# Seven gathered slots instead of six, and a scaling in four pieces, in a graph network on one core

## The chip, the core and the metric

The kernel runs on one core of a Trainium2 chip. Its engines work side by side and in order, each on its own list of instructions: TensorE (PE) multiplies, VectorE (DVE) and ScalarE (ACT) work on elements, GpSimd (POOL) issues among others the indirect transfers that gather table rows by index, and SyncE (SP) issues plain transfers. They wait for each other through semaphores. The metric is the time of one execution on the device in microseconds, the median of the runs shown.

## What is computed

Three graph layers on 3125 nodes and 53125 edges (sorted by target `dst`), a residual and a norm, then a message layer over the same edges:

```python
for l in range(3):                      # _L0_gnn_ref
    neigh = segment_sum(h[src], dst) * inv_deg
    h = h @ Ws_self[l] + neigh @ Ws_neigh[l] + bs[l]      # relu but in the last
x = layernorm(x + h)
# _L1_gnn_ref, idx_i = src, idx_j = dst
hs, hv = xs @ w_in2f_s, xv @ w_in2f_v           # a row of 4*32 values for each node
s, v = hs[idx_j], hv[idx_j]                     # gathered for each edge
Wij = (ssp(f_ij @ W1 + b1) @ W2 + b2) * rcut_ij
edge = products of s, v, the edge's angles Yr_ij and Wij
agg = segment_sum(edge, idx_i)                  # then two small products, ssp between
x = layernorm(x + out)
```

## The kernel before

Nodes are cut into TILES = 25 tiles of TN = 125. **First pass** (25 steps): products of tile and weights, and dense count matrices from the edges. **Three passes** of 25 steps each, k = 0 to 74 (AGGS = 75): TensorE multiplies the counts of tile k (25 blocks of 125 x 125, loaded into `abuf`) with the table of all nodes' rows (50 matmuls with 512 columns, L1208), and the products of the next layer lie between them. VectorE first scales the counts of tile k+1 in place, `scale(k + 1, 0)` at L1687, one operation over 3125 elements except at the first tiles of a pass, where `parts_of` (L575) cuts it. TensorE waits for a piece through `s_as` and `scaled_at`, which follows the written list SCALES (L566). In the third pass (k from 50) VectorE also takes moments (L1743 to L1763), norms (L1768, `normed`) and adds the residual (L1757); the normed rows give one tile a step of `msg_table`, which SyncE stores (L642) and counts in `s_rows`.

The edges were sorted by the tile of `src` into `by_src` during the second and third pass: each of 25 source tiles has a window of 128 partitions x SLOTS = 18 slots, sorted by `dst` within. A slot is thus a column of 128 edges, and its rows are gathered by one indirect transfer from `msg_table` by the edges' `dst`.

**Early gathers.** At the end of k = 50 POOL loads the window columns 0 to 5 of all tiles (L928, three transfers) and columns 6 to 11 of tile 0 (L926), copies the indices (L933, L934), and VectorE finds how many table tiles each slot needs (`early_max`, L1709 on, and `early_need`). TensorE waits for the maxima at k = 52, a = 4 (L1195). POOL then works through 30 steps (j, c): slot j of the five tiles of chunk c, five gathers (`gather_slot`, L937) into one of three buffers, and a store of the step before to `early_rows` (L951). A last step gathers the second group (slots 6 to 11) of tile 0 and stores it to `second_rows` (L960).

**Message stage.** For each source tile t there are NG = 3 groups of GS = 6 slots. VectorE's `group(t, g)` waits for TensorE's filters (L1220) and for the group's rows in `msg_slots[t % 2]`, makes products (L1991 first, then L1994, L1996, L2000, L2004, L2006); ScalarE scales (`scaled`, L1466), and TensorE sums (`sums`, L1242). Group 0's rows come from `early_rows` in one load (SyncE L814; ScalarE L1447 for tile 0), tile 0's group 1 from `second_rows` (L818), and all the others POOL gathers in the open (`gather`, L910), 12 a tile, 6 for tile 0, in order of tile and group, after all of `msg_table` has been stored. It may run two tiles ahead (`s_gd`).

Of the kernel before, what the change touches and what calls it, by code (L numbers as in the profile page):

```python
# [11 lines left out]
P = 128  # L12
# [12 lines left out]
SECOND = GS * CHUNKS  # L25
# [68 lines left out]
def gnn_kernel(nc, x, src, dst, src_n, pay, ws, wn, bs, w_in, w1, b1, w2, b2, wf1, wf2, out):  # L94
# [17 lines left out]
    early_rows = nc.dram_tensor("early_rows", [GS, CHUNKS, P, FEW * G], F32).ap()  # L112
    second_rows = nc.dram_tensor("second_rows", [P, GS * G], F32).ap()
# [58 lines left out]
    e_rows = [early.take(P, [GS, G]) for _ in range(3)]  # L172
    e_idx = early.take(P, [TILES, GS], I32)
    e_second = early.take(P, [GS], I32)
    e_f = early.take(P, [GS, TILES])
    e_fs = early.take(P, [GS])
    e_max = early.take(P, [GS + 1])
    e_most = early.take(1, [GS + 1])
    e_below = early.take(1, [GS + 1, TILES])
    e_need = early.take(1, [GS + 1], I32)  # L180
# [97 lines left out]
    e_win = ereg.take(P, [TILES, GS, PAY])  # L278
    e_swin = ereg.take(P, [GS, PAY])
# [128 lines left out]
    s_second = sem("second_group_loaded")  # L408
# [58 lines left out]
    def early_gathered(s):  # L467

        return 16 * sum(GS if n == SECOND else FEW for n in range(s % 3, s + 1, 3))

    def slots_gathered(t, g):

        if g == 0:
            return 16 * (t // 2 + 1)
        return 16 * GS * (t // 2 + (0 if g == 1 and t % 2 == 0 else 1))
# [99 lines left out]
    def parts_of(k):  # L575

        return {0: (0, 22, 23, 24, 25), 1: (0, 23, 25)}.get(k % TILES, (0, 25))

    with nc.Block() as block:

        @block.sync
        def _(sp):
# [147 lines left out]
            for k in range(AGGS):  # L730
# [44 lines left out]
                if k == AGGS - 4:  # L775
                    sp.wait_ge(s_eidx, len(PARTS_OF) + 1)
# [29 lines left out]
            def load_early(t):  # L806
                if t >= 2:
                    sp.wait_ge(s_gd, 3 * NG * (t - 2) + 3)
                c, i = t // FEW, t % FEW
                if t == 1 or i == 0:  # L810
                    for j in range(GS):
                        s = early_step(j, c)
                        sp.wait_ge(s_est[s % 3], loads_of(s, 3))
                sp.dma_start(msg_slots[t % 2][:, 0:GS, :], early_rows[:, c, :, i * G:(i + 1) * G].rearrange("j p k -> p j k")).then_inc(s_g[0][t % 2], 16)  # L814

            extras(sp, extra_round)
            sp.wait_ge(s_est[SECOND % 3], loads_of(SECOND, 3))
# [1332 lines left out]
```

## Time and profile before

| | us |
|---|---|
| median of 3 runs | 1892.74 (1888.39 to 1895.12) |
| the profiled execution | 1891.2 |
| its span | 1889.4 |
| PE busy | 1827.0 (97%) |
| DVE busy | 1180.4 (62%) |
| POOL busy | 1180.8 (62%) |
| ACT busy | 627.3 (33%) |

Times in the profile are from the start of the span. A "busy" share is an average over stages with different limits; the stage has to be looked at by itself. In a timeline a row gives start and duration of an instruction (or of several in a row, x6), and in brackets how long its engine had been idle and what ended that. "issue" is idle time for which the profile shows no releaser. The third pass runs from about 1142 to 1452, the message stage from 1457 to the end.

### The profile page before, as it was taken

What the parts mean: (1) busy time and instruction counts of PE and PEld (TensorE: products, weight loads), DVE (VectorE), ACT (ScalarE), POOL (GpSimd) and SP (SyncE); (2) the same over time, 40 slices, a digit from 0 to 9 for tenths busy, and PEclk for the clock granted to TensorE, in tenths of its full rate; (3) what the DMA queues carried; (4) which work ended last, traced back from release to release, by engine and by line L of the source; (5) the groups of instructions that cost most, each with busy time, mean ns of one, the idle gap of its engine ahead of it and who ended that gap; (6) DMA issues with size and microseconds to landing.
All of it is one profiled execution on the core that took longest, in us unless ns stands there. A gap on an engine that the chain in (4) does not pass through costs nothing. (4 is left out here: it accounts for less than half of the span.)

```text
span 1889.4 us, 23661 instructions
## 1 busy us (share of the span) xinstructions
PE 1827.0 (97%) x8259; PEld 1160.8 (61%) x8259; DVE 1180.4 (62%) x1811; ACT 627.3 (33%) x1432; POOL 1180.8 (62%) x1082
## 2 busy tenths in 40 slices
PE   7999999999999999999999998999998999999997
PEld 3454455555555555555555555666666888888886
DVE  5766678677644344343343344555553899999997
ACT  1566632233000000000000000111103888888885
POOL 4400000165588888888888883788886777777773
PEclk9999999999999999999999999999998999999999
DMA  5365566443454435444444434555564344434442
GB/s 156 108 218 182 202 217 185 124 115 104 129 143 138 123 107 147 134 134 124 117 130 122 114 98 156 179 190 195 195 196 133 89 116 116 113 108 107 108 117 56
DMA packets 235894, 261.88 MB, mean 139 GB/s; under 512 B 130678, under 2 KB 173280, under 8 KB 235773
## 3 DMA queue, kind: packets, MB, share of 16 engines
q1 hardware_dynamic: 200956, 204.29, 35.6%
q0 software_dynamic: 34032, 55.66, 11.0%
q8 instruction: 67, 1.10, 0.3%
q10 hardware_dynamic: 784, 0.39, 0.1%
q14 instruction: 55, 0.44, 0.1%
HBM read 172.52 MB, written 87.69 MB: 138 GB/s over the span
## 5 line engine op out<-in xcount | busy, mean ns | idle before, releaser
L1208 PE MATMUL low<-table,abuf 125*125 125x512 f16 x3750 | 835.2, 380 | 0.0
L1208 PEld LDWEIGHTS low<-table,abuf 125*125 125x125 bf16 x3750 | 506.4, 137 | 303.0 <-issue 27.9
L905 POOL DMA_INDIRECT by_src<-scat_row,sort x416 | 502.7, 1208 | 126.1 <-issue 118.8
L1037 PE MATMUL mid<-wbuf,h_t 128*125 128x512 f32 x1200 | 557.2, 601 | 14.0 <-DVE st_out L1733 10.9
L910 POOL DMA_INDIRECT table<-msg_table,wbuf x294 | 316.8, 1078 | 97.8 <-issue 97.5
L1037 PEld LDWEIGHTS mid<-wbuf,h_t 128*125 128x125 f32 x1200 | 214.9, 189 | 222.1 <-issue 198.2
L1743 DVE SCALAR_TENSOR_TENSOR y<-low,inv_deg,st_in 125x512 f32<-125x512 f32 x75 | 56.2, 749 | 446.6 <-PE low L1208 328.1
L1687 DVE TENSOR_TENSOR abuf<-abuf,row_scale 125x3125 bf16<-125x3125 bf16 (+4 forms) x87 | 256.9, 2956 | 1.2 <-DMA abuf<-adj 1.2
L937 POOL DMA_INDIRECT sort<-msg_table,sort x156 | 202.0, 1295 | 63.9 <-issue 47.2
L888 POOL TENSOR_TENSOR sort<-sort 128x416 f32<-128x416 f32 x26 | 31.8, 1224 | 329.9 <-DVE sort L1805 329.9
L1242 PE MATMUL low<-table,wbuf 128*125 128x256 f32 x900 | 209.9, 383 | 21.0 <-ACT table L1466 20.9
L1242 PEld LDWEIGHTS low<-table,wbuf 128*125 128x125 f32 x900 | 167.7, 189 | 50.1 <-DVE table L2006 25.1
L1419 ACT ACTIVATE y<-y 125x512 f32<-125x512 f32 x48 | 30.2, 629 | 437.7 <-DVE y L1743 437.7
L1332 ACT ACTIVATE table<-mid,row_inv_i 125x512 f16<-125x512 f32 x75 | 51.2, 683 | 314.2 <-DVE row_inv_i L1698 314.1
L1343 ACT ACTIVATE table<-top 125x500 bf16<-125x500 f32 (+1 forms) x175 | 120.4, 691 | 94.3 <-PE top L1068 94.2
L1466 ACT ACTIVATE table<-table,wbuf 128x128 f32<-128x128 f32 x450 | 139.3, 388 | 36.1 <-DVE table L1996 36.1
L1220 PE MATMUL mid<-w_sb,wbuf 97*128 97x384 f32 (+2 forms) x450 | 112.7, 387 | 2.4 <-issue 2.4
L1068 PEld LDWEIGHTS top<-table 128*128 128x128 bf16 x625 | 49.0, 98 | 77.6 <-issue 70.0
L1706 DVE SCALAR_TENSOR_TENSOR table<-mid,row_inv_i,table 125x512 f16<-125x512 f32 x75 | 56.3, 751 | 52.1 <-ACT table L1332 52.1
L1733 DVE TENSOR_TENSOR st_out<-mid,bias 125x512 f32<-125x512 f32 x75 | 51.4, 685 | 53.3 <-issue 49.9
L1220 PEld LDWEIGHTS mid<-w_sb,wbuf 97*128 97x128 f32 x450 | 69.4, 194 | 23.5 <-issue 3.8
L1662 DVE TENSOR_TENSOR table<-sort,node_iota 128x3200 bf16<-128x3200 bf16 (+1 forms) x45 | 81.8, 1855 | 2.0 <-ACT sort L1351 1.9
(244 smaller groups left out, 1616.6 us busy)
## 6 DMA issues: line engine op xcount, KB each, us to landing
abuf<-adj SPq DMA_DIRECT2D x75, 781.2 KB, 5.0
adj<-table SPq DMA_DIRECT2D x25, 781.2 KB, 4.5
states<-st_out SPq DMA_DIRECT2D x75, 256.0 KB, 2.3
st_in<-states SPq DMA_DIRECT2D x75, 256.0 KB, 4.9
flips<-y_flip SPq DMA_DIRECT2D x48, 256.0 KB, 4.3
h_t<-flips SPq DMA_DIRECT2D x192, 64.0 KB
early_rows<-sort POOLq DMA_DIRECT2D x30, 320.0 KB, 2.7
table<-early_rows SPq DMA_DIRECT2D x24, 384.0 KB, 6.5
```

What stands on the lines that cost most here:

```text
L905: pool.indirect_dma_start(out=by_src, out_offset=bass.IndirectOffsetOnAxis(ap=place_i[:, k * PIECE + j:k * PIECE + j + 1], axis=0), in_=sc ...
L910: pool.indirect_dma_start(out=rows[:, j, :], out_offset=None, in_=msg_table[:, :], in_offset=bass.IndirectOffsetOnAxis(ap=win[:, j, PAY_DS ...
L937: pool.indirect_dma_start(out=e_rows[s % 3][:, j, :], out_offset=None, in_=msg_table[:, :], in_offset=bass.IndirectOffsetOnAxis(ap=idx, ax ...
L1037: last = pe.matmul(to[0:TN, :], h_t[i % 2][:, k, 0:TN], weights[l % 2][:, a, k, :], start=k == 0, stop=k == KC - 1)
L1208: last = pe.matmul(p_agg[k % 2][0:TN, :], a_tile[k % 3][:, a, :], table[ps % 2][0:TN, a, h, :], start=a == 0 and h == 0, stop=a == TILES - ...
L1220: last = pe.matmul(w[:, (b * BLK + lo) * G:(b * BLK + hi) * G], filters[b], w2_sb[:, lo:hi, :].rearrange("k a b -> k (a b)"), start=True, ...
L1242: last = pe.matmul(p_acc[0:TN, :], hot32[:, g * GS + j, :], msg[n % 2][:, j, :], start=g == 0 and j == 0, stop=g == NG - 1 and j == GS - 1)
L1343: act.activation(to, of, ACT.Copy).then_inc(s_blke, 1)
L1466: last = act.activation(msg[n % 2][:, j, 0:G], av[n % 2][:, j, F:F + G], ACT.Copy, scale=win_p[t % 3][:, g * GS + j, PAY_Y:PAY_Y + 1])
L1662: return dve.tensor_tensor(to.rearrange("p b (n a) -> p b n a", a=PAIR), column.unsqueeze(2).broadcast_to([P, BLOCKS, n, PAIR]), node_iota ...
L1687: dve.tensor_tensor(a_tile[k % 3][:, lo:hi, :], a_tile[k % 3][:, lo:hi, :], row_scale[k // TILES % 2][0:TN, lo:hi].unsqueeze(2).broadcast_ ...
L1706: dve.scalar_tensor_tensor(out=table[l % 2][0:TN, t, 1, :], in0=n, scalar=row_inv[0:TN, 0:1], in1=table[l % 2][0:TN, t, 0, :], op0=ALU.mul ...
```

## The change

- `EARLY = 7`: early gathers take slots 0 to 6 of every tile, 35 steps of five gathers. The step for tile 0's second group, `second_rows`, `e_second`, `e_fs`, their load, copy, cast, reduction and semaphore go away.
- `load_early(t)` brings seven slots in one transfer, and waits for group 1 of tile t-2 where it waited for group 0, because slot 6 belongs to group 1.
- In the message stage POOL gathers slots 7 to 17 of every tile, tile 0 too: 11 a tile. Group 1's count of five gathers a tile is `2 * GS - EARLY`.
- `parts_of(k)` for k > 51 has four parts (0, 7, 13, 19, 25) in place of one. Part 0 keeps its place, part 1 follows before `normed`, part 2 before `add_residual`, part 3 behind it.

```diff
-SECOND = GS * CHUNKS
+EARLY = 7
+STEPS = EARLY * CHUNKS
...
+    def parts_of(k):
+
+        return {0: (0, 22, 23, 24, 25), 1: (0, 23, 25)}.get(k % TILES, (0, 7, 13, 19, 25) if k > 2 * TILES else (0, 25))
+
+    def later_parts(k):
+
+        return range(1, 4) if 2 * TILES + 1 < k < AGGS else range(0)
...
+        SCALES += [(k + 1, part) for part in later_parts(k + 1)]
...
             def load_early(t):
                 if t >= 2:
-                    sp.wait_ge(s_gd, 3 * NG * (t - 2) + 3)
+                    sp.wait_ge(s_gd, 3 * (NG * (t - 2) + 1) + 3)
...
-            pool.dma_start(e_swin, edges_of[:, 0, GS:2 * GS, :]).then_inc(s_ewin[0], 16)
             for n, (lo, hi) in enumerate(PARTS_OF):
                 pool.dma_start(e_win[:, lo:hi, :, :].rearrange("p t j k -> p t (j k)"),
-                               edges_of[:, lo:hi, 0:GS, :].rearrange("p t j k -> p t (j k)")).then_inc(s_ewin[n], 16)
+                               edges_of[:, lo:hi, 0:EARLY, :].rearrange("p t j k -> p t (j k)")).then_inc(s_ewin[n], 16)
...
-            steps_of = [(j, c) for j in range(GS) for c in range(CHUNKS)]
+            steps_of = [(j, c) for j in range(EARLY) for c in range(CHUNKS)]
...
-            need = pool.value_load(e_need[0:1, GS:GS + 1], min_val=1, max_val=TILES)
-            wait_alone(pool, s_rows, need)
-            gather_second()
             store_early(*steps_of[-1])
-            store_second()
...
-                for g in range(1 if t else 2, NG):
+                for g in range(1, NG):
                     if t >= 2:
                         pool.wait_ge(s_gd, 3 * (NG * (t - 2) + g) + 3)
-                    for j in range(g * GS, (g + 1) * GS):
+                    for j in range(max(g * GS, EARLY), (g + 1) * GS):
                         gather(msg_slots[t % 2], win_p[t % 3], j, s_g[g][t % 2])
...
+                for part in later_parts(k + 1)[0:1]:
+                    scale(k + 1, part)
                 if k > 2 * TILES:
                     normed(k - 1)
...
+                for part in later_parts(k + 1)[1:2]:
+                    scale(k + 1, part)
                 if ps == 2:
                     add_residual(k)
+                for part in later_parts(k + 1)[2:3]:
+                    scale(k + 1, part)
```

## Rows read from the trace of the kernel before

**Rows 1.** Windows: length, then busy time per engine, PE clock, DMA share.

```profile
1168.00:1420.00 252.00, 252.00 (x1294) 170.41 (x1293) 131.47 (x153) 26.48 (x83) 195.87 (x164) 0.99 0.56 183
1450.00:1500.00 50.00, 44.32 (x209) 36.84 (x210) 35.67 (x59) 35.73 (x91) 32.45 (x30) 0.83 0.41 116
1650.00:1700.00 50.00, 47.68 (x272) 41.03 (x271) 48.40 (x88) 42.01 (x115) 39.03 (x37) 1.00 0.42 110
```

**Rows 2.** Groups by line, 1550 to 1800: count, busy us, mean ns, idle before.

```profile
L910 POOL DMA_INDIRECT table<-msg_table,wbuf x181 | 195.5, 1080 | 55.2 <-issue 55.2
```

**Rows 3.** Timeline of a steady tile: start, duration, engine, line, idle before.

```profile
1671.66 0.75 DVE L1991 TENSOR_TENSOR table<-table,wbuf 128x576 f32<-128x576 f32 x1
...
1673.58 1.86 ACT L1466 ACTIVATE table<-table,wbuf 128x128 f32<-128x128 f32 x6 [0.87 <-DVE table L1996]
...
1675.58 2.83 PE L1242 MATMUL low<-table,wbuf 128*125 128x256 f32 x12 [0.77 <-ACT table L1466]
...
1679.56 1.47 PE L1220 MATMUL mid<-w_sb,wbuf 97*128 97x384 f32 x6
...
1681.06 0.76 DVE L1991 TENSOR_TENSOR table<-table,wbuf 128x576 f32<-128x576 f32 x1 [0.33 <-PE mid L1220]
...
1681.87 0.95 POOL L910 DMA_INDIRECT table<-msg_table,wbuf  x1 [0.30 <-issue]
...
1688.29 0.75 DVE L1991 TENSOR_TENSOR table<-table,wbuf 128x576 f32<-128x576 f32 x1
```

**Rows 4.** Timeline of the message stage's first tiles.

```profile
1462.34 2.77 PE L1220 MATMUL mid<-w_sb,wbuf 97*128 97x384 f32 x6
...
1464.83 0.95 POOL L910 DMA_INDIRECT table<-msg_table,wbuf  x1 [0.30 <-issue]
...
1469.94 2.08 POOL L910 DMA_INDIRECT table<-msg_table,wbuf  x1 [0.30 <-issue]
...
1470.46 0.74 DVE L1991 TENSOR_TENSOR table<-table,wbuf 128x576 f32<-128x576 f32 x1
...
1483.48 1.13 POOL L910 DMA_INDIRECT table<-msg_table,wbuf  x1 [0.30 <-issue]
...
1487.53 0.76 DVE L1991 TENSOR_TENSOR table<-table,wbuf 128x576 f32<-128x576 f32 x1 [2.03 <-issue]
```

**Rows 5.** Groups by line, 1168 to 1450, third pass.

```profile
L937 POOL DMA_INDIRECT sort<-msg_table,sort x156 | 202.0, 1295 | 63.9 <-issue 47.2 <-SPq L773 16.8
L951 POOL DMA_DIRECT2D early_rows<-sort x30 | 17.5, 584 | 0.0
...
L1687 DVE TENSOR_TENSOR abuf<-abuf,row_scale 125x3125 bf16<-125x3125 bf16 x22 | 75.0, 3407 | 0.0
```

**Rows 6.** Timeline of one scaling and the gather beside it.

```profile
1386.85 3.41 DVE L1687 TENSOR_TENSOR abuf<-abuf,row_scale 125x3125 bf16<-125x3125 bf16 x1
...
1387.46 3.61 POOL L937 DMA_INDIRECT sort<-msg_table,sort  x1 [0.31 <-issue]
1390.17 0.54 DVE L1768 TENSOR_SCALAR table<-y,mv,rstd 125x512 f32<-125x512 f32 x1
```

**Rows 7.** End of the early gathers: timeline, chain (start, us, what), timeline.

```profile
1450.27 0.77 POOL L960 DMA_DIRECT2D second_rows<-sort  x1 [1.19 <-DMA sort<-msg_table,sort]
...
1454.97 2.31 DMA msg_table<-msg_row
...
1459.57 1.01 POOL L910 DMA_INDIRECT table<-msg_table,wbuf  x1 [8.53 <-issue]
```

**Rows 8.** Start of the third pass: chain of waits.

```profile
1156.71 8.61 DMA wbuf<-by_src
```

**Rows 9.** Transfers of the message stage: KB each, median us to landing.

```profile
table<-early_rows SPq DMA_DIRECT2D x24, 384.0 KB, 6.5
...
table<-early_rows ACTq DMA_DIRECT2D x1, 384.0 KB, 3.6
```

**Rows 10.** L1991 alone: what ended VectorE's idle time before it (us, times).

```profile
  issue: 3.4, 4
```

More of the change, by code:

```diff
@@ L171, in gnn_kernel @@
     early = Region(sort_sb[:, :], 7 * CH * 4)
[L172 to L180, printed above, removed]
+    e_rows = [early.take(P, [FEW, G]) for _ in range(3)]
+    e_idx = early.take(P, [TILES, EARLY], I32)
+    e_f = early.take(P, [EARLY, TILES])
+    e_max = early.take(P, [EARLY])
+    e_most = early.take(1, [EARLY])
+    e_below = early.take(1, [EARLY, TILES])
+    e_need = early.take(1, [EARLY], I32)
     x_rows = Region(sort_sb[:, :], 7 * CH * 4).take(P, [SLOTS, G])
@@ L277, in gnn_kernel @@
     ereg = Region(wbuf[:, :, :].rearrange("p a k -> p (a k)"), 2 * 2 * KC * D * 4)
-    e_win = ereg.take(P, [TILES, GS, PAY])
-    e_swin = ereg.take(P, [GS, PAY])
+    e_win = ereg.take(P, [TILES, EARLY, PAY])
     treg = Region(tbuf[0][:, :], T_SIZE)
@@ L467, in early_gathered @@
     def early_gathered(s):
-        return 16 * sum(GS if n == SECOND else FEW for n in range(s % 3, s + 1, 3))
+        return 16 * FEW * (s // 3 + 1)
     def slots_gathered(t, g):
-        if g == 0:
-            return 16 * (t // 2 + 1)
-        return 16 * GS * (t // 2 + (0 if g == 1 and t % 2 == 0 else 1))
+        return 16 * (t // 2 + 1) * {0: 1, 1: 2 * GS - EARLY}.get(g, GS)
     def node_rows(t):
@@ L915, in extra_round @@
                 wait_alone(pool, s_xl, q * 32)
-                for s in range(SECOND - 2, SECOND + 1):
+                for s in range(STEPS - 3, STEPS):
                     pool.wait_ge(s_est[s % 3], loads_of(s, 3))
@@ L951, in store_early @@
                 pool.dma_start(early_rows[j, c, :, :].rearrange("p (t k) -> p t k", t=FEW), e_rows[s % 3][:, 0:FEW, :]).then_inc(s_est[s % 3], 16)
-            def gather_second():
-                pool.wait_ge(s_est[SECOND % 3], loads_of(SECOND - 3, 3))
-                for j in range(GS):
-                    gather_slot(SECOND, j, e_second[:, j:j + 1])
-            def store_second():
-                pool.wait_ge(s_eg[SECOND % 3], early_gathered(SECOND))
-                pool.dma_start(second_rows.rearrange("p (j k) -> p j k", j=GS), e_rows[SECOND % 3]).then_inc(s_est[SECOND % 3], 16)
             pool.wait_ge(s_eneed, 1)
-            steps_of = [(j, c) for j in range(GS) for c in range(CHUNKS)]
+            steps_of = [(j, c) for j in range(EARLY) for c in range(CHUNKS)]
             for n, (j, c) in enumerate(steps_of):
@@ L1193, in _ @@
                         pe.wait_ge(s_emax, 1)
-                        for n in range(GS + 1):
+                        for n in range(EARLY):
                             top = pe.transpose(p_b[n // 4][0:1, n % 4 * P:(n % 4 + 1) * P], e_max[:, n:n + 1], ident[:, :])
@@ L1443, in _ @@
             act.wait_ge(s_acc, AGGS)
-            for j in range(GS):
+            for j in range(EARLY):
                 s = early_step(j, 0)
                 act.wait_ge(s_est[s % 3], loads_of(s, 3))
-            act.dma_start(msg_slots[0][:, 0:GS, :], early_rows[:, 0, :, 0:G].rearrange("j p k -> p j k")).then_inc(s_g[0][0], 16)
+            act.dma_start(msg_slots[0][:, 0:EARLY, :], early_rows[:, 0, :, 0:G].rearrange("j p k -> p j k")).then_inc(s_g[0][0], 16)
             def hots(t):
```

35 lines of the change are left out of this document (11 added, 24 removed).

## Prediction

> **What bounds the kernel now.** I read the windows first. Through the third pass TensorE is busy 252.00 of 252.00 us, and GpSimd (POOL), which gathers rows there for later, is not what the pass waits for. In the message stage VectorE is busy 48.40 of 50 us, TensorE 47.68, POOL 39.03 [rows 1]. The chain of waits of the page gives 15% of the span to POOL's gathers at L910, so the next question is whether POOL paces the stage. The grouped view makes it look so: 181 gathers in 250 us, busy 195.5, idle 55.2 and all of that "issue", which is 0.305 us behind every gather, never a wait [rows 2].
>
> The timeline of one steady tile says otherwise [rows 3]. The last gather of tile 13's third group is issued at 1681.87 and used at 1688.29, 6.42 us later (7.52 us for the second group). Where a group really waits for its gather, the distance is 4.05 us (issued 1483.48, used 1487.53, VectorE idle 2.03 before it) [rows 4]. So in the steady part rows lie ready 2.4 us before use. What repeats every 16.63 us (L1991 at 1671.66 and at 1688.29) is another loop: VectorE's product lets ScalarE scale (1673.58, 1.86 us), then TensorE sums (1675.58, 2.83), hidden layer and filters (1679.56, 1.47) release VectorE's L1991 at 1681.06 after an idle 0.33, and VectorE works on without a pause to the next turn. POOL keeps the same 16.63 us because VectorE's operations hold it up: 12 gathers x 1.255 is 15.06, and holds fill the rest. POOL follows; it doesn't lead.
>
> **Third pass: gathers added.** 175 gathers in 35 steps stand for 156 in 31 (30 steps of five and one of six). A gather undisturbed costs 0.95 + 0.305 = 1.255, a store 0.584 + 0.3 = 0.88 [rows 5]. Added: 19 x 1.255 + 4 x 0.88 = 23.8 + 3.5 = 27.4 us of POOL.
>
> **Third pass: scaling in four.** The 156 gathers were busy 202.0 us; 156 x 0.95 is 148.2, so 53.8 us are holds, 2.4 for each of 22 scalings of 3.41 us [rows 5]. How a hold looks: the scaling L1687 runs 1386.85 to 1390.26, the gather issued at 1387.46 ends at 1391.07, 0.81 after it [rows 6]. After the change the pieces hold 875 and 750 elements; at 3.41 us for 3125 they are about 0.97 and 0.84 us, 3.5 together. VectorE's order becomes piece, piece, L1768, piece, L1757, piece, some 4.3 us in a row. The question is whether a held gather gets in between two of them or waits for all. In rows 6 L1768 (1390.17, 0.54) stands right behind the scaling; had the gather waited for it too, it would have ended at 1391.5, not 1391.07. It got in between, and so it does in all 19 cases of this kind. Then the first gather is held up to 0.97 us, the next, 1.1 us behind the end of an operation, meets the tail of one: some 0.6 to 1.0 us a step, 13 to 22 in all. If the two pieces that follow each other directly count as one (no row shows this pair), 1.7 us at the first and up to 38 in all. I take 20. POOL: +27.4 + 20 - 53.8 = -6 us (ends: -13 and +12).
>
> What this is worth: POOL ended this work at 1451.04 (1450.27 + 0.77) and then sat idle 8.53 us, because the last row of the table landed only at 1457.28 (1454.97 + 2.31); the first gather of the message stage came at 1459.57 [rows 7]. So earlier is worth nothing, and up to 6.2 us later costs nothing: **0 us**, at most 6 at the far end. TensorE gets three more waits a step, about 70; it is busy 252.00 of 252.00 with the waits it has, so 0 (bound: 0 to 1.5 us). The pieces end 1.1 us later than the one operation did, and five microseconds of VectorE's idle time follow, so TensorE's next tile doesn't see them. L1768, now ahead of two pieces, comes 1.5 us sooner and nobody is waiting for it: 0. VectorE's fixed cost of three more operations, 0.1 to 0.2 us a step, goes into the same idle time.
>
> The Trainium skill, SBUF — State Buffer, section Who interferes with whom, says that a VectorE operation with two SBUF inputs contends with a GpSimd instruction that reads SBUF, which the 19 held gathers bear out. The same section also reports `tensor_tensor` as not stalling DMAs; by that the holds would have another cause, and the split would give nothing (rival 2).
>
> **Start of the third pass.** TensorE and VectorE wait there for POOL's indices: transfers from by_src, 8.61 us from issue to the last landing, on the chain of waits [rows 8]. Bytes grow from 156 to 175 slot columns (12%): up to +1.0 us. The first of four issues falls away, and so do two small VectorE operations (L1712, L1714). No row here has their price; on VectorE nothing in this profile is under 0.15 us, so I take 0.9 for the three (0.5 for an issue like the 0.58 of a store [rows 5], 0.2 each for the others): -0.9. Sum +0.1, bounds -0.9 to +1.0.
>
> **Message stage, steady part.** POOL issues 11 gathers a tile, not 12. By rows 3 nobody waited for the twelfth: 0 us over tiles 5 to 23. The load of the seven slots now waits for the second group of tile t-2, not the first, some 5.4 us later on SyncE (a third of 16.63). Behind it in that queue stands the window load of tile t+1, which waits for the third group's sums of that same tile t-2 and so still comes later; and from there to the use in tile t are almost two tiles, over 24 us, for a load of 6.5 us [rows 9]. Hidden; if that cover were gone, 6.5 us a tile. The load on ScalarE's queue for tile 0 grows by a sixth: it took 3.6 us from 1454.91, so it lands near 1459.1 where 1458.5 was [rows 9], and VectorE starts at 1460.03 after TensorE's filters. Hidden by 0.9 us.
>
> **Message stage, first tiles: here it costs.** Before, tile 0's second group was ready in second_rows. Now POOL gathers five of its slots in the open, and until tile 5 it has more to do than before (11 + 11t gathers against 6 + 12t). I walk it with rows 4 and 7.
> - Tile 0, second group: fifth gather issued 1464.83, + 4.05 = 1468.9.
> - Tile 0, third group: six more gathers, 7.5 us, issued about 1472.4, landed 1476.5. It was used at 1470.46, so +6.0.
> - Tile 1, second group: ScalarE, TensorE's sums, hidden and filters come behind that, as in rows 3: still +6.0.
> - Tile 1, third group: VectorE's own work reaches it 5.4 us later, at 1491.5; its gathers (the 22nd) land near 1490.9. It was used at 1487.53 after the 2.03 us wait, which is now swallowed: +4.0.
> - Tile 2, third group: moves by the same 4.0. Its 33rd gather lands over 2 us before VectorE gets there. From here nobody waits for gathers any more. Before, L1991 had four waits of this kind, 3.4 us together [rows 10]; the first was the 2.03, so the three later ones are worth -1.3.
>
> That is **+2.7 us**. While TensorE waits for tile 0's second group it stands idle some 3.6 us at a moment when its clock is still mostly down (0.83 of full over 1450 to 1500 [rows 1]; the filters took 2.77 us there against 1.47 at 2.4 GHz [rows 3, 4]). Staying longer at 1.2 GHz costs from 0 to 4.1 us (one round of filters, hidden layer and sums at the slow rate, 1.3 + 1.3 + 1.5). I take 0.6, nearer to none, because most of that round then lies beside waiting for gathers.
>
> **Sum.** 0 + 0.1 + 0 + 2.7 + 0.6 = +3.4 us. The profiled execution took 1891.2 us (span 1889.4 and 1.8 around it): 1894.6 after. That execution lies 1.5 below the median of the three runs, 1892.74, so the median after should be **1896** (0.18% more). About 0.3%, 5.7 us, is what a measurement of this kernel can tell from no change.
>
> **Rivals.**
> 1. *No measurable change, slightly slower* (the forecast), 1896, own range 1890 to 1901. Chance 0.64.
> 2. *The third pass hands the delay on* (slower). If the pieces in a row hold POOL as one, or the holds aren't the scaling's, nothing of the 53.8 us is saved and POOL ends at 1451.04 + 27.4 = 1478.4. It decides from 1457.3 on: 21 us late, and VectorE can't catch up at 16.63 a tile. 21 + 2.7: 1916. Against it: 19 gathers that got in behind the scaling. One gather at 1469.94 that took 2.08 us, held by two operations in turn [rows 4], speaks for it. Chance 0.06.
> 3. *The first tiles cost more* (slower by over 0.3%): low clock until tile 1 (+4.1 for +0.6), or POOL ready only at 1461 (+4). 1900 to 1903. For it: the clock in rows 1; against: most of that slow round lies beside waiting for gathers. Chance 0.18.
> 4. *POOL paces the stage after all* (faster). The page's chain and the unbroken row of gathers speak for it, the 6.42 us against it. With 11 gathers a tile would fall to VectorE's busy time, 48.40 / 50 x 16.63 = 16.1: 0.5 us over 20 tiles, -10, and with +3.4 at the start 1886. Chance 0.12.
>
> **How the numbers follow.** The time is the likeliest case's. The range 1886 to 1904 takes in rivals 3 and 4 and leaves out rival 2 and the tails. Faster by over 0.3%: 0.12 (rival 4 and a little of case 1's lower end, less rival 4's weaker half). Slower by over 0.3%, above 1898.4: rivals 2 and 3 and a little of case 1's upper end, 0.24. Between: 0.64.
>
> **What would show each step.** In the profile after: four L1687 forms of about 0.97 and 0.84 us a step; L937's mean near 1.07 us over 175; POOL's idle before the first L910 still several us and that gather within 0.5 us of its old distance from the last table row; L1991 of tile 0's second group some 3.7 us and of its third some 6 us after their old places; the steady distance of L1991 still 16.63; last gathers issued 8 us and more before use. A steady distance below 16.6 makes me wrong towards rival 4; a first L910 without idle before it, towards rival 2.

## The result, and the profile after

| | before | after |
|---|---|---|
| median, us | 1890.97 (1887.51 to 1896.0, 20 runs) | 1896.09 (1892.62 to 1900.13, 20 runs) |
| ratio to before | | 1.0031 (95%: 1.0022 to 1.004) |
| span of the profiled execution | 1889.4 | 1894.2 |
| POOL busy | 1180.8 | 1150.1 |

The kernel became slower by 0.31%, 4.2 to 7.6 us by the interval. The 1896 us of the prediction is met, but two of its terms were too small and a high starting value made up for them, as the step-by-step account below shows. Seven of the runs told of below fell on two chips on which every program, the kernel before too, stopped for microseconds at changing places; of those only stretches without a stop are read. In the kernel after the lines have moved: L910 is now L907, L937 is L931, L951 is L945, L1687 is L1668, L1768 is L1747, L1757 is L1736, L1991 is L1973, L1220 is L1201, L1242 is L1223, L1466 is L1447, L1447 is L1428, L1052 is L1033.

**Third pass.** Groups by line of the kernel after, 1168 to 1455 (count, busy us, mean ns, idle before), to be read against [rows 5]. A "hold" is the time by which a gather takes longer than its undisturbed 0.95 us.

```profile
L931 POOL DMA_INDIRECT sort<-msg_table,sort x175 | 189.2, 1081 | 69.1 <-issue 52.7 <-SPq L772 16.2 <-DMA early_rows<-sort 0.3
L945 POOL DMA_DIRECT2D early_rows<-sort x35 | 20.4, 583 | 1.3 <-DMA sort<-msg_table,sort 1.2
L1668 DVE TENSOR_TENSOR abuf<-abuf,row_scale 125x750 bf16<-125x750 bf16 x66 | 62.0, 939 | 0.8
L1668 DVE TENSOR_TENSOR abuf<-abuf,row_scale 125x875 bf16<-125x875 bf16 x22 | 23.4, 1064 | 0.0
```

There are 19 gathers more and yet 12.8 us less busy time: the mean fell from 1295 to 1081 ns. 175 x 0.95 is 166.3, so 22.9 us of holds are left of 53.8. On VectorE the pieces cost more than their share of the elements, 0.94 and 1.06 us, together 3.88 for the 3.41 of the one operation. One step of the kernel after, on VectorE and POOL, shows how a gather gets through (start, duration, engine, line, idle before):

```profile
1388.05 1.91 DVE L1668 TENSOR_TENSOR abuf<-abuf,row_scale 125x875 bf16<-125x875 bf16 x2
1389.88 0.54 DVE L1747 TENSOR_SCALAR table<-y,mv,rstd 125x512 f32<-125x512 f32 x1
1390.33 0.94 DVE L1668 TENSOR_TENSOR abuf<-abuf,row_scale 125x750 bf16<-125x750 bf16 x1
1391.18 0.68 DVE L1736 TENSOR_TENSOR st_in<-st_in,st_out 125x512 f32<-125x512 f32 x1
1391.90 0.94 DVE L1668 TENSOR_TENSOR abuf<-abuf,row_scale 125x750 bf16<-125x750 bf16 x1
```

```profile
1387.84 0.95 POOL L931 DMA_INDIRECT sort<-msg_table,sort  x1 [0.30 <-issue]
1389.09 1.69 POOL L931 DMA_INDIRECT sort<-msg_table,sort  x1 [0.30 <-issue]
1391.09 1.60 POOL L931 DMA_INDIRECT sort<-msg_table,sort  x1 [0.31 <-issue]
```

The gather of 1389.09 starts in the second piece, which ends at 1389.96, and ends at 1390.78, 0.82 us later, although L1747 stood right behind the piece: it got in between. The gather of 1391.09 did not. It starts 0.18 us before the end of the third piece (1391.27) and ends at 1392.69, 0.83 us after L1736, which stands behind that piece. Each has about a quarter of the hold of [rows 6]: 0.74 and 0.65 us where 2.66 were.

Both kinds recur over the pass. Also where a piece stands directly behind a piece, all five gathers that started in the first of the two ended 0.82 to 0.92 us behind that first one. But 13 gathers that started near the end of the third piece, 12 of them in its last 0.2 us, were held by L1736 as well.

**End of the early gathers.** POOL's timeline in the kernel after, against [rows 7]:

```profile
1446.80 0.57 POOL L945 DMA_DIRECT2D early_rows<-sort  x1 [1.22 <-DMA sort<-msg_table,sort]
1459.07 1.01 POOL L907 DMA_INDIRECT table<-msg_table,wbuf  x1 [11.70 <-issue]
```

POOL ends at 1447.37, 3.7 us before its old 1451.04, and idles 11.70 us in place of 8.53.

**First tiles.** The first products of tiles 0 and 1 on VectorE in the kernel after; before, the first five stood at 1460.03, 1465.15, 1470.46, 1474.91 and 1480.12, and tile 1's third group at 1487.53 [rows 4]:

```profile
1460.07 0.76 DVE L1973 TENSOR_TENSOR table<-table,wbuf 128x576 f32<-128x576 f32 x1 [7.91 <-PE mid L1201]
...
1467.73 0.76 DVE L1973 TENSOR_TENSOR table<-table,wbuf 128x576 f32<-128x576 f32 x1 [3.15 <-DMA table<-msg_table,wbuf]
...
1476.70 0.76 DVE L1973 TENSOR_TENSOR table<-table,wbuf 128x576 f32<-128x576 f32 x1 [3.58 <-PE mid L1201]
...
1480.28 0.75 DVE L1973 TENSOR_TENSOR table<-table,wbuf 128x576 f32<-128x576 f32 x1
...
1488.39 0.76 DVE L1973 TENSOR_TENSOR table<-table,wbuf 128x576 f32<-128x576 f32 x1 [1.34 <-PE mid L1201]
...
1493.71 0.74 DVE L1973 TENSOR_TENSOR table<-table,wbuf 128x576 f32<-128x576 f32 x1
```

The shifts are +0.04, +2.58, +6.24, +5.37, +8.27 and +6.18 us. The last gathers of tile 0's second and third group on POOL, and TensorE in the same stretch:

```profile
1464.86 0.95 POOL L907 DMA_INDIRECT table<-msg_table,wbuf  x1 [0.30 <-issue]
...
1472.54 1.41 POOL L907 DMA_INDIRECT table<-msg_table,wbuf  x1 [0.31 <-issue]
```

```profile
1469.15 1.47 PE L1201 MATMUL mid<-w_sb,wbuf 97*128 97x384 f32 x6
...
1474.98 1.47 PE L1201 MATMUL mid<-w_sb,wbuf 97*128 97x384 f32 x6
1480.63 5.11 PE L1223 MATMUL low<-table,wbuf 128*125 128x256 f32 x12 [4.18 <-ACT table L1447]
```

The bracket before 1476.70 names TensorE, but the filters of tile 0's third group (1469.15, 1.47 us) were over at 1470.62; those of 1474.98 are tile 1's. The group's last gather was issued at 1472.54, 4.16 us before the use. The gathers set this start. Tile 1's second group at 1488.39, by contrast, starts when its filters are over, and these stand on TensorE behind tile 0's last sums. Those took 5.11 us behind an idle time of 4.18; [rows 3] has 2.83 for sums. The windows say why (length, then busy time of PE, PEld, DVE, ACT and POOL, PE clock, DMA share, GB/s). After:

```profile
1470.00:1482.00 12.00, 6.77 (x31) 5.11 (x30) 8.36 (x14) 6.64 (x20) 9.56 (x9) 0.85 0.35 86
1482.00:1492.00 10.00, 10.00 (x46) 8.15 (x44) 6.76 (x13) 6.71 (x16) 7.56 (x9) 0.84 0.35 89
```

and before:

```profile
1470.00:1482.00 12.00, 12.00 (x66) 10.30 (x65) 10.77 (x19) 9.34 (x22) 9.78 (x8) 1.00 0.37 109
1482.00:1492.00 10.00, 8.40 (x47) 6.75 (x46) 7.90 (x14) 7.49 (x23) 7.95 (x7) 1.00 0.20 48
```

The granted clock falls back from 2.4 GHz during the idle time of 1476.45 to 1480.63: stretches of 2 us have 1.00 from 1476, 0.61 from 1478, 0.50 from 1480 and from 1482, 0.69 from 1484 and 1.00 again from 1486. The sums thus run at 1.2 GHz for the most part. Before the second group's sums TensorE had stood idle for only 1.05 us, and the clock stayed up (0.98 from 1468 to 1472).

**Steady part.** POOL's gathers in the kernel after, 1550 to 1800, against [rows 2], and the first line of the page's chain that ended last:

```profile
L907 POOL DMA_INDIRECT table<-msg_table,wbuf x173 | 187.4, 1083 | 63.2 <-issue 49.7 <-DVE table L1982 12.8 <-DVE table L1973 0.6
```

```profile
PE 23%; DVE 10%; ACT 3%; issue 2%; DMA 1%; POOL 1%; DVEq 0%; POOLq 0%; ACTq 0%
```

POOL now has waits for free buffers (on VectorE's L1982 and L1973), and the chain gives it 1% where it gave 15%. The period is 16.63 us as before. From the last issue to the use of a third group it is 23 us (tile 13 on) in place of the 6.42 of [rows 3]. The shift of the first products is +6.61 us by tile 2's third group and shrinks from there, by 0.53 us at tile 3, 0.69 at tile 4 and 0.38 at tile 24, where the kernel before waited for gathers, and ends at +4.96.

### The profile page after: what moved, and what is told of

Read it like the earlier page. It is cut to its first block and busy times, and to the rows that moved or that the text cites. A ratio compares the mean times of both kernels' runs of the same rounds, so it can differ in the third digit from the quotient of the medians.

```text
span 1894.2 us, 23732 instructions
## 1 busy us (share of the span) xinstructions
PE 1827.6 (96%) x8259; PEld 1161.4 (61%) x8259; DVE 1186.6 (63%) x1878; ACT 627.1 (33%) x1432; POOL 1150.1 (61%) x1084
## 5 line engine op out<-in xcount | busy, mean ns | idle before, releaser
L907 POOL DMA_INDIRECT table<-msg_table,wbuf x275 | 297.5, 1082 | 109.5 <-issue 91.3
L1668 DVE TENSOR_TENSOR abuf<-abuf,row_scale 125x750 bf16<-125x750 bf16 (+6 forms) x156 | 265.7, 1718 | 1.5 <-DMA abuf<-adj 0.7
L1223 PE MATMUL low<-table,wbuf 128*125 128x256 f32 x900 | 212.5, 386 | 23.5 <-ACT table L1447 23.4
L931 POOL DMA_INDIRECT sort<-msg_table,sort x175 | 189.2, 1081 | 69.1 <-issue 52.7
L1223 PEld LDWEIGHTS low<-table,wbuf 128*125 128x125 f32 x900 | 169.4, 191 | 53.8 <-DVE table L1988 27.4
L1447 ACT ACTIVATE table<-table,wbuf 128x128 f32<-128x128 f32 x450 | 139.3, 388 | 38.3 <-DVE table L1978 38.3
L1201 PE MATMUL mid<-w_sb,wbuf 97*128 97x384 f32 (+2 forms) x450 | 112.7, 387 | 2.5 <-issue 2.5
L1687 DVE SCALAR_TENSOR_TENSOR table<-mid,row_inv_i,table 125x512 f16<-125x512 f32 x75 | 56.3, 750 | 52.6 <-ACT table L1313 52.6
L1201 PEld LDWEIGHTS mid<-w_sb,wbuf 97*128 97x128 f32 x450 | 69.4, 194 | 23.5 <-issue 3.8
```

Source lines behind the costliest of these rows:

```text
L907: pool.indirect_dma_start(out=rows[:, j, :], out_offset=None, in_=msg_table[:, :], in_offset=bass.IndirectOffsetOnAxis(ap=win[:, j, PAY_DS ...
L931: pool.indirect_dma_start(out=e_rows[s % 3][:, j, :], out_offset=None, in_=msg_table[:, :], in_offset=bass.IndirectOffsetOnAxis(ap=idx, ax ...
L1201: last = pe.matmul(w[:, (b * BLK + lo) * G:(b * BLK + hi) * G], filters[b], w2_sb[:, lo:hi, :].rearrange("k a b -> k (a b)"), start=True, ...
L1223: last = pe.matmul(p_acc[0:TN, :], hot32[:, g * GS + j, :], msg[n % 2][:, j, :], start=g == 0 and j == 0, stop=g == NG - 1 and j == GS - 1)
L1447: last = act.activation(msg[n % 2][:, j, 0:G], av[n % 2][:, j, F:F + G], ACT.Copy, scale=win_p[t % 3][:, g * GS + j, PAY_Y:PAY_Y + 1])
L1668: dve.tensor_tensor(a_tile[k % 3][:, lo:hi, :], a_tile[k % 3][:, lo:hi, :], row_scale[k // TILES % 2][0:TN, lo:hi].unsqueeze(2).broadcast_ ...
```

## The experiments

Theory A is the prediction's walk: the time is lost at tile 0, because the rows of its second group are gathered in the open, and TensorE's clock adds to it. The rivals are those of the prediction, and that the loss comes with something else that was changed.

A measure used below beside the totals is the length of the message stage in the profiled execution, from the first product of tile 0 to that of tile 24's third group. It leaves out what differs by execution ahead of the stage (see the last section). Before it is 1868.35 - 1460.03 = 408.3 us, after 413.2. It is not free of chance either: the split alone, below, has before's code in this stage and 406.6 us.

The totals of the runs on the two disturbed chips, with the number of executions:

| | us | the kernel before on that chip, us |
|---|---|---|
| fewer gathers in front of tile 0 | 1974.04 (6) | 2009.26 (17) |
| fewer gathers in the steady part | 1934.51 (4) | 2009.26 (17) |
| another order on TensorE, kernel before | 2022.68 (12) | 2009.26 (17) |
| the same with tile 0's second group kept | 1993.92 (6) | 2009.26 (17) |
| this last one again | 2074.69 (6) | 2037.41 (11) |
| another order, kernel before, again | 2038.06 (6) | 2037.41 (11) |
| the changed kernel once more | 2092.81 (6) | 2037.41 (11) |

Executions of the kernel before alone range there from 1992 to 2056 us and from 2029 to 2330, so that these totals decide nothing.

### Tile 0's second group gathered early again

```diff
+            for j in range(REST):
+                gather_slot(STEPS, j, e_second[:, j:j + 1])
             store_early(*steps_of[-1])
...
+            pool.dma_start(second_rows..., e_rows[STEPS % 3])
...
-                for g in range(1, NG):
+                for g in range(1 if t else 2, NG):
```

REST is 2 * GS - EARLY = 5; the load, indices, maxima and semaphore of this step come back with it.

> The changed kernel, but tile 0's slots 7 to 11 are gathered early again, as a last step of five gathers with its own store and load (seven slots of every tile stay early, the scaling stays in four). Theory A (the cost is only that these five gathers moved into the open): VectorE's L1991-like product of tile 0's groups comes within 0.3 us of its place in the kernel before, the wait of 2.0 us in tile 1's third group shrinks to under 1 us because POOL is one gather ahead there, tiles 3 and 4 and the last tile wait no more; about 5 us under the changed kernel and lost 2 to 3 us more: 1888.5, 2 to 3 us under the kernel before. Theory B (seven slots early or four pieces cost something by themselves, in the third pass or through the larger loads): no better than the kernel before, 1891 to 1893.

Measured: 1890.66 us (11 runs), ratio to before 0.9999 (0.9986 to 1.0012). First products of tile 0's three groups in this kernel:

```profile
1462.78 0.76 DVE L1998 TENSOR_TENSOR table<-table,wbuf 128x576 f32<-128x576 f32 x1 [9.18 <-PE mid L1221]
1467.90 0.76 DVE L1998 TENSOR_TENSOR table<-table,wbuf 128x576 f32<-128x576 f32 x1 [0.60 <-PE mid L1221]
1473.20 0.75 DVE L1998 TENSOR_TENSOR table<-table,wbuf 128x576 f32<-128x576 f32 x1
```

Their distances, 5.12 and 5.30 us, are those of before (5.12 and 5.31), and the long waits are gone. The seven slots, the wider loads, the moved wait on SyncE and the split are all still in. So the loss is tile 0's second group; what the rest of the change costs or gains is too small for the totals (-0.14 to +0.12%). The total lies between the 1888.5 us of theory A and the 1891 to 1893 of theory B and decides neither; the places of the first products do, for A. In the profile the stage is 405.7 us long, 2.6 less than before: the wait of tile 1's third group is 1.02 us in place of 2.03, and those of tiles 3, 4 and the last are gone. But the split alone (below), which has before's gathers, has 406.6: there the gather that took 2.08 us in [rows 4] took 1.41, and the wait of 2.03 us behind it is missing. Single profiles can't tell a gain of this size from chance.

### The seven slots without the split

```diff
-        return {...}.get(k % TILES, (0, 7, 13, 19, 25) if k > 2 * TILES else (0, 25))
+        return {...}.get(k % TILES, (0, 25))
```

> The changed kernel with the scaling of a tile in one operation, as before; seven slots early. Theory A (one long operation holds a gather for 2.4 us, four short ones in a row let it in between): the 175 early gathers are busy about 225 us instead of 189, POOL ends them near 1478 instead of 1447, the first gather of the message stage comes near 1480 instead of 1459, and the run takes 17 to 22 us more than the changed kernel: about 1915. Rival (holds have another cause, so that the split gave nothing): gathers busy 189, time as the changed kernel, 1896.

Measured: 1915.21 us (4 runs), ratio 1.0121 (1.0092 to 1.015). Rival 2 of the prediction had 1916 for a split that saves nothing. POOL's last store of the early gathers with its first gather of the message stage, and the first products of tile 0's first two groups in this kernel:

```profile
1480.12 0.57 POOL L945 DMA_DIRECT2D early_rows<-sort  x1 [1.23 <-DMA sort<-msg_table,sort]
1482.13 1.01 POOL L907 DMA_INDIRECT table<-msg_table,wbuf  x1 [1.44 <-issue]
```

```profile
1464.43 0.76 DVE L1973 TENSOR_TENSOR table<-table,wbuf 128x576 f32<-128x576 f32 x1 [10.95 <-DMA table<-early_rows]
1489.81 0.76 DVE L1973 TENSOR_TENSOR table<-table,wbuf 128x576 f32<-128x576 f32 x1 [20.87 <-DMA table<-msg_table,wbuf]
```

The 175 gathers are busy 221.2 us, 54.9 more than 175 x 0.95, the same holds as before (53.8). The scalings are thus what holds the gathers, and the split is what pays for the seventh slot.

### The split alone, in the kernel before

```diff
-        return {...}.get(k % TILES, (0, 25))
+        return {...}.get(k % TILES, (0, 7, 13, 19, 25) if k > 2 * TILES else (0, 25))
```

with the calls of `scale(k + 1, part)` as in the change.

> The kernel before with the scaling in four pieces and nothing else. Theory A: the 156 gathers are busy about 170 us instead of 202, POOL ends some 30 us earlier (near 1420) and then idles longer, the message stage begins at the same place, time unchanged within 1 us of the kernel before. Rival (the pieces, their waits on TensorE, or the earlier norm move the third pass): the pass moves by more than 1 us either way, at most +1.5 from the waits.

Measured: 1889.88 us (11 runs), ratio 0.9997 (0.9983 to 1.0012). The group of early gathers in this kernel, and POOL's first gather of the message stage:

```profile
L942 POOL DMA_INDIRECT sort<-msg_table,sort x156 | 170.4, 1092 | 63.5 <-issue 47.2 <-SPq L778 16.4
```

```profile
1459.97 1.01 POOL L915 DMA_INDIRECT table<-msg_table,wbuf  x1 [38.78 <-issue]
```

POOL is 31.6 us less busy (202.0 - 170.4), and nearly all of it becomes idle time, 38.78 us for 8.53. Neither the earlier end of POOL nor the 0.47 us a step that VectorE works more moves the time by what the totals can tell (about 3 us).

### TensorE kept busy during the wait

```diff
...
+                if t == 0:
+                    for _ in range(8):
+                        pe.matmul(p_low[1][:, 0:2 * G], ident[:, :], zeros[:, :], start=True, stop=True)
                 sums(t, 2)
```

> The changed kernel with eight extra matmuls (128 columns of ident against 256 of zeros, into a bank that is free then) before tile 0's last sums, where TensorE stood idle 4.18 us and its next twelve matmuls then took 5.11 us instead of 2.83. Theory A (idle time brings the clock down to 1.2 GHz, and that costs 2.3 us of the 5 lost): the sums take 2.8 us, tile 1's second group comes 2.0 to 2.3 us sooner, time 1.5 to 2.3 us under the changed kernel. Rival (the slower sums lie beside other waiting): the sums are fast and the time stays within 0.7 us of the changed kernel.

Measured: 1896.91 us (12 runs), ratio 1.0032 (1.0018 to 1.0045), no difference to the changed kernel (1.0031) that the totals can tell; the 1.5 to 2.3 us less that theory A had are not seen. The timeline of TensorE has what the total doesn't:

```profile
1477.37 1.47 PE L1201 MATMUL mid<-w_sb,wbuf 97*128 97x384 f32 x6
1478.67 3.62 PE L1296 MATMUL low<-zeros,ident 128*128 128x256 f32 x16
1483.16 2.83 PE L1223 MATMUL low<-table,wbuf 128*125 128x256 f32 x12 [0.87 <-ACT table L1450]
```

With 3.62 us of idle time filled, the sums take 2.83 us, not 5.11, and the clock granted from 1470 to 1482 is 0.99 (0.85 without). Counted from the first product of tile 0, tile 1's second group starts at +26.24 us where the changed kernel has +28.32 (before: +20.09), and tile 1's third group at +32.55 (after: +33.64), now behind a wait of 0.93 us for its gathers. The stage is 411.8 us long, 1.4 less. That the dip of the clock costs 2.1 us at tile 1's second group and that 1.0 of them comes back at the next wait for gathers is what these rows show; that it is worth 1.4 us in the end rests on one execution of each, and is no more than two executions of one stage differ by. The way through the start of the third pass (steps 48 to 54) took 3 us longer here than in the changed kernel's profile; such differences are in every total.

The run also shows the walk of the prediction without the clock. Tile 1's third group stands at +5.05 us against before (32.55 - 27.50), not at the +4.0 of the walk, and waits for its gathers, which the walk had landed before VectorE came.

### Fewer gathers in front of tile 0

```diff
...
+                    if t == 0 and g == 1:
+                        pool.dma_start(msg_slots[0][:, 2 * GS - 3:2 * GS, :], msg_table[0:3 * P, :]...).then_inc(s_g[1][0], 16)
-                    for j in range(max(g * GS, EARLY), (g + 1) * GS):
+                    for j in range(max(g * GS, EARLY), (g + 1) * GS - (3 if t == 0 and g == 1 else 0)):
```

> The changed kernel, but of the five row gathers that tile 0's second group needs at the start of the message stage, three are replaced by one plain transfer of 384 other rows on the same queue (left out: the right rows for three slots of tile 0). Theory A (the 5 us are the late gathers of tile 0, one after the other on GpSimd): GpSimd gives 0.9 us for the plain transfer instead of 4.1 us for three gathers, so every later gather starts 3.2 us earlier. Tile 0's second group then waits for nothing (+0 against the kernel before instead of +2.6), its third group starts at about +3.0 instead of +6.2, TensorE's idle time before tile 0's last sums shrinks under 2 us and they run at full clock (2.8 us, not 5.1), tile 1's third group stands at +1.0 to +1.5 instead of +6.2, and the end at +0.5: 1891.5 us (1890 to 1893). Rival B (the loss comes with the wider seven-slot loads or the moved waits on SyncE, not with the count of gathers): unchanged, 1896.

VectorE's wait for the second group is set to the new count. POOL and VectorE of this kernel up to tile 0's third group, a stretch without a stop:

```profile
1521.85 0.78 POOL L967 DMA_DIRECT2D table<-msg_table  x1 [69.59 <-issue]
1524.87 1.02 POOL L907 DMA_INDIRECT table<-msg_table,wbuf  x1 [2.24 <-issue]
1526.20 1.36 POOL L907 DMA_INDIRECT table<-msg_table,wbuf  x1 [0.30 <-issue]
...
1534.41 1.41 POOL L907 DMA_INDIRECT table<-msg_table,wbuf  x1 [0.30 <-issue]
```

```profile
1523.05 0.76 DVE L1975 TENSOR_TENSOR table<-table,wbuf 128x576 f32<-128x576 f32 x1 [8.95 <-PE mid L1203]
1529.61 0.76 DVE L1975 TENSOR_TENSOR table<-table,wbuf 128x576 f32<-128x576 f32 x1 [2.04 <-DMA table<-msg_table,wbuf]
1538.58 0.76 DVE L1975 TENSOR_TENSOR table<-table,wbuf 128x576 f32<-128x576 f32 x1 [3.58 <-issue]
```

I had mis-sized the replacement: behind the plain transfer POOL stood still for 2.24 us (why stays open), so that not 3.2 us but 1.1 were saved. The last gather before the third group comes 11.36 us after tile 0's first product (1534.41 - 1523.05), where the changed kernel has 12.47 (1472.54 - 1460.07). The third group starts at +15.53 in place of +16.63: 1.10 us for 1.11, one to one, and the second group's wait shrinks by the same 1.1. The sizes expected were missed, TensorE's idle time of 4.18 us and slow sums (5.46 us) among them; that the products follow the gathers held, and wider loads or moved waits (rival B) would have left them in place.

### Fewer gathers in the steady part

```diff
...
-                    for j in range(g * GS, (g + 1) * GS):
+                    for j in range(g * GS, g * GS + (2 if g == 2 and t >= 3 else GS)):
```

> The kernel before, but from tile 3 on the third group gathers two slots instead of six (left out: four slots' rows per tile keep those of an earlier tile). GpSimd then has 8 gathers a tile in place of 12, 4 x 1.3 us less in a period of 16.63 us. Theory A (VectorE and its wait of 0.32 us for TensorE set the period, GpSimd is not the pace): the period stays 16.63 us to 0.03, only the short waits for gathers in tiles 3, 4 and 24 (0.46, 0.59, 0.30 us) go, 1889.5 us. Rival 4 of the prediction (GpSimd paces the stage): the period falls, by up to 1 us a tile, 1870 to 1885 us.

VectorE's waits are set to the new count. From tile 3 on this execution had no stop. With eight gathers a tile in place of twelve, 16 of 21 periods are 16.62 us and five 16.63, the idle 0.32 us before every second group is still there, and POOL, busy 130.9 of 250 us, waits. This settles rival 4: GpSimd doesn't pace the stage. Its chance of 0.12 hung on the chain's 15% and on POOL's unbroken row of gathers. The low total of this run is no sign against it: up to tile 3 the code is before's, and from there on the period is.

### The changed kernel once more

> The changed kernel itself, a second profiled execution. It tells what of the comparison belongs to the kernel and what to one execution. Theory A: against the start of tile 0's first product, tile 0's second and third group start at +7.7 and +16.6 us, the second group of tile 1 at +28.3 us, the last tile's third group at +413.2 us, to 0.3 us; the period is 16.63 us; 1896 us. What may differ by execution, by up to 1.5 us each: the start-up, the start of the third pass, and the clock of the last message product of the third pass. Rival B (those offsets differ by execution as well, and a part of the 5 us is chance): offsets off by 1 us and more.

Up to tile 0's third group this execution is free of stops:

```profile
1586.81 0.76 DVE L1973 TENSOR_TENSOR table<-table,wbuf 128x576 f32<-128x576 f32 x1 [9.16 <-PE mid L1201]
1594.52 0.76 DVE L1973 TENSOR_TENSOR table<-table,wbuf 128x576 f32<-128x576 f32 x1 [3.19 <-DMA table<-msg_table,wbuf]
1603.45 0.76 DVE L1973 TENSOR_TENSOR table<-table,wbuf 128x576 f32<-128x576 f32 x1 [3.55 <-issue]
```

+7.71 and +16.64 us against +7.66 and +16.63 in the first one. The two waits are the kernel's, not chance. Whether the later groups' offsets repeat, +28.3 us behind the slow sums among them, couldn't be tested.

### Another order on TensorE

The period of 16.63 us holds an idle 0.32 us of VectorE, waiting for the second group's filters, which TensorE makes behind the next tile's hidden layer [rows 3]. I turned the two round, in the kernel before (twice) and in the kernel with tile 0's second group kept (three times):

```diff
...
+                filters(t, 1)
                 if t + 1 < TILES:
                     hidden(t + 1)
-                filters(t, 1)
                 sums(t, 0)
```

> The kernel before, with one order changed on TensorE: a tile's second filters are made ahead of the next tile's hidden layer, not behind it. In the trace of before the second group's first product waits 0.32 us for these filters in 22 tiles and 0.60 us in tile 0. Theory A (the period is VectorE's work, 16.3 us, plus this wait): the wait goes, 24 x 0.32 = 7.7 us, 1883.5 us. Rival B (ScalarE takes over: its activations of the hidden layer come 1.3 us later and it has no idle time behind them, so the third group's products wait as long): 1890 to 1893 us, and the 0.32 us stands before the third group instead.

> The changed kernel with tile 0's slots 7 to 11 gathered early as well (as in the experiment that kept the second group) and with TensorE's changed order. Theory A: the two gains add up: 1890.7 less 7.7 us, 1883 us (1881 to 1885), and 0 to 2 us under the kernel before with that order alone. Rival B as for the order alone: 1889 to 1892 us.

> The changed kernel with tile 0's slots 7 to 11 gathered early as well and with TensorE's changed order (a tile's second filters ahead of the next tile's hidden layer), once more on a calm chip. In the first look the undisturbed tiles had a period of 16.50 to 16.54 us and not 16.63: the wait of 0.32 us before the second group had gone, and the third group stood 0.27 us later. Theory A (ScalarE's later activations take back two thirds of the gain): period 16.50 us, 24 x 0.13 = 3.1 us less than the same kernel without the new order, 1887 to 1888 us. Rival B (the 7.7 us of the waits are gained in full): 1883 us. Rival C: no gain, 1890 to 1891 us.

> The kernel before with TensorE's changed order alone, once more on a calm chip. Theory A: period 16.50 us in place of 16.63, 1887.5 to 1889 us. Rival B: 1883.5 us. Rival C (the third group's gathers, six slots behind a distance of 6.4 us, now come late and the period stays 16.6 us): 1890 to 1892 us.

In the second of these four six tiles without a stop had a period of 16.50 to 16.54 us; in the other three there were too few such tiles to rest on, so what the order alone is worth in the kernel before stays open.

> The changed kernel with tile 0's slots 7 to 11 gathered early as well and with TensorE's changed order, a third time, since the chips of the two earlier looks were disturbed. Theory A: the wait of 0.32 us before the second group goes, 0.27 us of it come back before the third group through ScalarE's later activations, the period is 16.50 us in place of 16.63, and the time 3 us under that of the same kernel without the new order: 1887 to 1888 us, ratio to before 0.998. Rival B (the waits are gained in full): period 16.31 us, 1883 us. Rival C (no gain): 1890 to 1891 us.

Measured, on a chip without such stops: 1889.44 us (12 runs), ratio to before 0.9988 (0.9976 to 1.0). The period is 16.49 to 16.51 us in 18 of the 21 tiles from 3 on. VectorE in one of them:

```profile
1652.17 0.75 DVE L1998 TENSOR_TENSOR table<-table,wbuf 128x576 f32<-128x576 f32 x1
...
1657.13 0.75 DVE L1998 TENSOR_TENSOR table<-table,wbuf 128x576 f32<-128x576 f32 x1
...
1661.01 0.95 DVE L1875 SCALAR_TENSOR_TENSOR wbuf<-wbuf 96x768 f32<-96x768 f32 x1 [0.21 <-ACT wbuf L1403]
```

The wait before the second group is gone, and 0.21 us stand now before L1875, which needs ScalarE's hidden layer. Theory A is right on the mechanism and the period. On the total the size is not confirmed: 1887 to 1888 us were expected, the gain against the kernel before lies between 0 and 4.5 us, and against this kernel without the new order (0.9999) it can't be told from none. In the profile the stage is 404.7 us long against 405.7: 0.13 us a tile gained, some of it spent in a wait of 2.17 us at tile 1's third group. It is faster than the changed kernel (0.9988 against 1.0031), and hardly faster than the kernel before.

## Why the prediction was right, step by step

- **Third pass, POOL.** Holds of 20 us expected within 13 to 22, 22.9 measured; POOL 6 us earlier expected, 3.7 found, or 4.9 counted from the pass itself, which ran 1.2 us later. A little more than the range, because the pieces last 0.94 and 1.06 us and not 0.84 and 0.97, and because 13 gathers were held by L1736 behind the third piece as well: by the rows above 0.60 us each (1392.69 for 1392.09), an estimate of 8 of the 22.9. The decision that mattered, that a held gather gets in between two operations, was right for a full scaling (all 21 such gathers of the trace before, not only 19) and for the pair that no row had shown, but not for these 13. VectorE's three more operations cost 0.47 us a step, not 0.1 to 0.2, in idle time. The price of this term, 0, was right, and the seven slots without the split show the cliff beside it, 1915 us.
- **What holds the gathers.** Seven slots with the scaling in one piece had 54.9 us of holds, with it in four 22.9: it is the scaling. The Trainium skill, SBUF — State Buffer, section Who interferes with whom, has a two-input VectorE operation contend with GpSimd's SBUF reads, and the runs agree. The same section's remark that a probe showed `tensor_tensor` not stalling DMAs doesn't fit indirect gathers issued by GpSimd: each scaling in one piece held one for some 2.4 us.
- **Start of the third pass.** +0.1 us expected; between steps 48 and 54 the distance grew by 0.24, well within what executions differ by. The pieces that go away are in the trace of before after all: 0.58 us for the issue, 0.17 and 0.16 for the two operations, 0.9 together as assumed. The sum is not testable at this size.
- **Steady part.** 0, and 0: period 16.63 in both.
- **First tiles.** Tile 0's third group +6.0, measured +6.24. The second group came at +2.58, not at +3.8: its use followed the last issue (1464.86) by 2.87 us and not by 4.05. The distance of 4.05 was taken from a third group; for the third group it held (4.16). The error had no effect, since the third group waited anyway.
- **The walk at tile 1: a term that was too small.** The walk landed the gathers of tile 1's third group before VectorE came, at 1.31 us a gather (landings from 1476.5 to 1490.9 for eleven). In the kernel after the eleven gathers from 1472.54 to 1488.17 took 1.42 us each, since VectorE's operations hold them here too. Behind the slow sums of the kernel after that is hidden. With TensorE kept busy the group waited 0.93 us for its gathers and came at +5.05, not +4.0, and the stage was 3.5 us over before's, not 2.7.
- **The clock: the other term that was too small.** I took 0.6 us, arguing that most of the slow round lies beside waiting for gathers. Tile 0's last sums took 5.11 us for 2.83, 2.3 more, and all of it stood on the path: tile 1's second group came at +8.27 where I had +6.0, its third group at +6.18 for +4.0, and there its rows had been issued 5.5 us before. With TensorE kept busy the stage is 1.4 us shorter: that is the clock's price in the end, in one execution of each. I had the wrong pause in mind: before the second group's sums TensorE waited 1.05 us and the clock stayed up; it falls in the 4.18 us before the third group's.
- **Later waits.** -1.3 expected, -1.6 measured (0.53 + 0.69 + 0.38).
- **Sum.** The walk gave +2.7 and the clock +0.6, 3.3 us for the stage; measured 4.9, about 0.8 more for each by the run with TensorE kept busy. Ahead of the stage I had +0.1 and the profiles show +0.04, though by chances that cancel: step 48 came 0.96 us later, and the third pass's last product with its transposes took 1.2 us less, at full clock. With the medians the loss is 5.1 us, the forecast 3.4. That the predicted 1896 came out to a tenth is luck: the three runs that I started from lay 1.8 us above the median of twenty.

## What to carry to other kernels

A phase change that moves work off a preparation which was hidden (tile 0's extra rows) into the open costs time once, here 5 us for five gathers, even where the steady part has room: prepare the first tile specially and let the rest share. Read the pace of a loop from the distance between issue and use, not from an engine's unbroken row of work or from its share in the chain of waits: that share went from 15% to 1% with the period unchanged. And where an engine is to wait longer than before, look at TensorE's clock behind that wait as a cost of its own: here 2.1 us for the group behind it.

## What the runs showed of the hardware

- A gather held by a VectorE operation ends 0.8 to 0.9 us after that operation. All 21 gathers held by a scaling in one piece got in before the operation that follows at once (0.81 to 0.90 us behind the scaling); in the kernel after the five in the pair of pieces did too (0.82 to 0.92). But 13 gathers that began near the end of the third piece were held by L1736 as well and took 1.57 to 1.89 us, and the gather of 1469.94 in the kernel before took 2.08. Cutting one operation of 3.41 us into four costs VectorE 0.47 us (3.88) and gives GpSimd 1.4 us back (31.6 us over 22).
- A plain transfer from the table issued by GpSimd ahead of gathers took 0.78 us, with 2.24 us of standstill behind it, against 0.305 behind a gather. Behind the stores between the early gathers there was no such standstill: in the kernel before one ran from 1381.53 for 0.58 us, and the next gather began at 1382.41.
- After the same idle time of 3.03 us on TensorE the last message product of the third pass ran at either level of the clock, by execution. In the kernel before and after:

```profile
1452.75 1.89 PE L1052 MATMUL mid<-w_in_sb,h_t 128*125 128x32 f32 x8 [0.68 <-ACT h_t L1328]
```

```profile
1453.57 1.06 PE L1033 MATMUL mid<-w_in_sb,h_t 128*125 128x32 f32 x8 [0.68 <-ACT h_t L1309]
```

Of seven executions it was slow in four (before, second group kept, TensorE kept busy, the last run) and fast in three (after, the split alone, the seven slots without it); with the transposes ahead of it this is 1.2 us that no edit made. The way from step 48 to step 54 took 98.8 us before, 99.0 after, 102.0 with TensorE kept busy and 94.3 in the last run, on code that is the same in all but the number of index columns and the split. Two single profiles of this kernel can therefore differ by several microseconds ahead of the stage one wants to compare. The stage has to be measured from its own start, and even so it differed by 1.7 us between the kernel before and the split alone, which share its code.
